# Products of probabilities and values issued for two key tiles together, in an attention and feed-forward block on one core

## The reference, cut to what matters

```python
x = x + attention(layernorm(x))          # x is 1 x 4096 x 256, float32
x = x + ffn_fp8(layernorm(x))            # 256 x 256 weight, rounded to fp8 values

def attention(x):                        # 16 heads of 16 columns, causal over 4096 rows
    q, k, v = split(x @ Wqkv_w + Wqkv_b)
    attn = softmax(q @ k.T * 0.25 + causal_mask)
    y_softmax = attn @ v
    # recurrence over the rows: state = retention*state + Gamma * outer(v_t, k_t)
    y_stp = scan(state, (q, k, v))       # y_t = (W_static + state) @ q_t
    alpha = sigmoid(gelu(x @ gate_w1 + gate_b1) @ gate_w2 + gate_b2)
    return (alpha * y_softmax + (1 - alpha) * y_stp) @ out_w + out_b
```

## Time and profile before

| | |
|---|---|
| median of three runs | 2258.62 us (2258.2 to 2261.62) |
| the profiled execution, span from first to last instruction | 2262.8 us |
| TensorE busy, share of the span | 2012.1 us, 89% |
| VectorE busy | 1911.7 us, 84% |
| ScalarE busy | 1258.6 us, 56% |
| GpSimd busy | 838.2 us, 37% |
| mean granted TensorE clock | 0.940 of full speed |

### The profile page before, as it was taken

How to read it: one execution, slowest core, us unless ns; L and a number is a source line. 1 busy time by engine, 2 the same in 40 slices (tenths; PEclk the granted TensorE clock), 3 DMA queues, 4 the chain that set the end, 5 groups by cost and what they waited for, 6 DMA issues and landing times. The chain is left out here.

```text
span 2262.8 us, 42161 instructions
## 1 busy us (share of the span) xinstructions
PE 2012.1 (89%) x11840; PEld 696.9 (31%) x11840; DVE 1911.7 (84%) x3051; ACT 1258.6 (56%) x2518; POOL 838.2 (37%) x843
## 2 busy tenths in 40 slices
PE   6876999999989999999898999989999999998543
PEld 3441233323323332333223333232332322222432
DVE  5656999998997999989987999898979898863677
ACT  3532166665655666666556666665656666766221
POOL 1320042433443433425342424253514242754435
PEclk9985599999999999999999999999999999999775
DMA  5987152251132622512235314221452111211702
GB/s 142 266 188 168 23 95 49 66 88 57 44 82 56 103 64 57 90 49 62 59 71 101 73 50 67 68 62 53 88 79 75 47 45 38 68 44 35 198 28 74
DMA packets 153963, 179.50 MB, mean 79 GB/s; under 512 B 62352, under 2 KB 100240, under 8 KB 153744
## 3 DMA queue, kind: packets, MB, share of 16 engines
q1 hardware_dynamic: 151360, 175.06, 33.2%
q10 hardware_dynamic: 2384, 1.77, 0.3%
HBM read 134.32 MB, written 42.21 MB: 78 GB/s over the span
## 5 line engine op out<-in xcount | busy, mean ns | idle before, releaser
L1004 DVE TENSOR_REDUCE pmax<-PS 128x1 f32<-128x512 f32 (+3 forms) x2304 | 1335.1, 635 | 181.9 <-PE PS L860 123.2
L971 ACT ACTIVATE probs<-PS 128x512 f32<-128x512 f32 (+3 forms) x2304 | 1118.0, 567 | 615.3 <-PE PS L878 481.6
L860 PE MATMUL PS<-K_st,Q_st 96*128 96x512 bf16 (+3 forms) x1408 | 502.3, 362 | 32.9 <-DVE pmax L1004 28.9
L878 PE MATMUL PS<-Q_st,K_st 98*128 98x512 bf16 (+3 forms) x1408 | 443.2, 361 | 16.5 <-ACT probs L971 11.3
L824 POOL COPY carry<-state 128x1 f32<-128x1 f32 x256 | 47.1, 184 | 1061.9 <-DVE state L1040 1061.9
L860 PE MATMUL PS<-K_first,Q_st 96*128 96x512 bf16 (+3 forms) x896 | 354.2, 411 | 64.9 <-DVE pmax L1004 34.0
L835 POOL TENSOR_TENSOR v_exp<-v_exp,k_rows 128x512 f32<-128x512 f32 x256 | 348.2, 1361 | 108.4 <-DMA v_exp<-qkv_t 108.2
L1040 DVE TENSOR_TENSOR_SCAN state<-retention,carry,v_exp 128x512 f32<-128x512 f32 x256 | 357.1, 1395 | 1.8 <-POOL v_exp L835 1.6
L899 PE MATMUL PS<-probs,V_g 128*17 128x512 f32 (+3 forms) x2816 | 343.5, 561 | 0.0
L826 POOL TENSOR_TENSOR state<-state,q_rows 128x512 f32<-128x512 f32 x256 | 330.5, 1291 | 20.6 <-POOL carry L824 0.2
L878 PE MATMUL PS<-Q_st,K_first 98*128 98x512 bf16 (+3 forms) x896 | 298.7, 373 | 7.2 <-issue 6.2
(11 more groups left out here) (124 smaller groups left out, 999.0 us busy)
## 6 DMA issues: line engine op xcount, KB each, us to landing
v_exp<-qkv_t SPq DMA_DIRECT2D x256, 256.0 KB
qkv_t<-proj SPq DMA_DIRECT2D x24, 512.0 KB, 3.5
qk_parts<-parts SPq DMA_DIRECT2D x24, 512.0 KB, 4.7
Q_st<-qk_parts SPq DMA_DIRECT2D x192, 64.0 KB, 3.9
K_first<-qk_parts SPq DMA_DIRECT2D x24, 320.0 KB, 12.6
K_st<-qk_parts SPq DMA_DIRECT2D x24, 320.0 KB, 13.6
K_st<-qk_parts SPq DMA_DIRECT2D x24, 192.0 KB, 6.8
v_rows<-vaug SPq DMA_DIRECT2D x32, 136.0 KB, 5.9
```

What stands on the lines that cost most here:

```text
L860: mm = pe.matmul(PS[:, bank, 0:width], Q_st[0:KS, c, h, j * P:(j + 1) * P], keys[0:KS, h, blk * CH:blk * CH + width], start=True, stop=(bl ...
L878: mm = pe.matmul(PS[:, bank, 0:CH - r * P], keys[:, h, kt * P:(kt + 1) * P], Q_st[:, c, h, r * P:CH], start=True, stop=(kt < TPC * c))
L971: act.activation(probs[:, tile % P_SLOTS, h, 0:CH - r * P], PS[:, item % S_BANKS, 0:CH - r * P], ACT.Exp, scale=SCALE).then_inc(exp_done, 1)
L1004: dve.tensor_reduce(pmax[:, s % 2, hj, blk:blk + 1], PS[:, S_BANKS + item % M_BANKS, 0:width], AX.X, ALU.max).then_inc(max_done, 1)
```

## The change

The planner keeps the tiles whose V is due in a list, and issues V for two tiles together. With tiles counted from 0, V of tiles t-2 and t-1 now stand after the fourth S of tile t for every even t from 2 on, and odd tiles have no V. `probs` gets a fourth buffer (8 KB more of each partition). The evacuation of a finished chunk (`out_evac`) and its turn stay behind the last V of the chunk; since all chunks have an even number of tiles, that V is issued in the same tile as before. At the end of a group the last two V are issued together, as before. V itself, its waits, and every other step are unchanged.

```diff
-P_SLOTS = 3
+P_SLOTS = 4
+TOGETHER = 2
...
-    pending = None
+    pending = []
+
+    def values_of(tiles):
+        for tile in tiles:
+            emit(("values", 0) + tile)
+            if tile[1] == KEY_TILES[tile[0]] - 1:
+                emit(("out_evac", 0, tile[0]), event=False)
+                if tile[0] < NCH - 1:
+                    turns.append([6, ("out_turn", 0, tile[0]), 5, ("out_norm", 0, tile[0])])
+
...
-            if pending:
-                emit(("values", 0) + pending)
-                if pending[1] == KEY_TILES[pending[0]] - 1:
-                    emit(("out_evac", 0, pending[0]), event=False)
-                    turns.append([6, ("out_turn", 0, pending[0]), 5, ("out_norm", 0, pending[0])])
-            pending = (s, kt)
+            if len(pending) == TOGETHER:
+                values_of(pending)
+                pending.clear()
+            pending.append((s, kt))
             max_items(share[GH])
     assert not slots and not todo
-    emit(("values", 0) + pending)
-    emit(("out_evac", 0, NCH - 1), event=False)
+    values_of(pending)
```

## The result

| | before | changed |
|---|---|---|
| median of the runs | 2260.12 us (four runs, 2258.2 to 2264.89) | 2401.09 us (four runs, 2392.57 to 2414.42) |
| ratio, 95% interval | | 1.062 (1.057 to 1.066) |
| span of the profiled execution | 2262.8 us | 2406.8 us (2408.49 us as a run) |

The change makes the kernel 6.2% slower. The forecast was 2368 us, range 2300 to 2408; the median lies in the range, near its upper end, and two of the four runs (2408.49 and 2414.42) lie above it.

The account below looks back on a forecast made before the run. TensorE was taken to bound pairs without units, VectorE the commoner pairs with them. Three full groups at +28 (+84) and the fourth at +25 gave +109 on the 2262.8 us span; the median forecast was 2368 us, range 2300 to 2408.

Parts of the forecast that it names:

- The loop: From the M behind one pair of V to the next, through VectorE and three banks: 6.95 us, 6.80 with narrow blocks.
- 32 pairs, unit on the odd tile, up to tile 72: Pairs in each group where VectorE runs dry across both V: +0.80 us each, less diagonal savings, +23 us.
- nine more beyond tile 80: Pairs in groups 1 to 3 with four M a tile and a unit on the odd tile alone: 0.7 each, +6 us.
- the fourth group: Last group: +22 up to tile 80 with bursts' saving, then ScalarE's loop adds +4; in all +25 us.
- pairs without a unit: 0: Pairs of tiles with no unit: TensorE's saving is used up by the loop, bounds -0.2 and +0.1 us.
- the -1 for the tiles behind the bursts: Tiles behind each burst, with four S and V and no M, keep the saved switch: 4 x 0.23, -1 us.
- these M are too few to bind the banks: Fourth group beyond tile 80: M mostly too few for the banks to bind, so ScalarE's loop does; +4 us on 28 pairs.
- more is late: Rival: late evacuations (28 us) or a lower clock from TensorE's longer waits, 2410 to 2440 us; chance 0.09.
- the rival that the pair is not cheaper: Rival: the second V has its own drain of 0.21 us, loop 7.01, 33 us more, 2401 us; chance 0.05.
- ScalarE's loop in the fourth group: Beyond tile 80, exponentials, S and both V form a loop of 5.42 us a pair, +0.12 to +0.15 on 28 pairs.
- Smaller loss: Rival: present stalls at narrow blocks, folds and turns are absorbed by VectorE's new idle time, 2300 to 2325 us; chance 0.17.
- TensorE's saving is the gain: Rival: VectorE never runs dry, so up to 61 us of saved switches come back, some 2198 or 2230 us; chance 0.07.

Follow-up runs that it names:

- pairs_at_units: Changed kernel with V paired only where a unit stands ahead of a tile with four M, elsewhere single: 2245.03 us, 0.992 of the kernel before.

## Why the prediction was right, and where it was off

The direction, the mechanism and its price per pair were right. The loop was forecast at 6.95 us for whole blocks and 6.80 on average; it is 6.90 in the rows above, and over the 32 pairs with a unit up to tile 72 the mean length is 6.75. (This and the sums below are from the starts of the first S of each tile; for each pair the shortest of its three occurrences in the full groups, which leaves most of the disturbances below aside.)

| a full group | forecast | measured |
|---|---|---|
| 32 pairs, unit on the odd tile, up to tile 72 | +23 | +24.9 |
| nine more beyond tile 80 | +6 | +6.4 |
| all other pairs | -1 | +2.4 |
| sum | +28 | +33.7 |
| the fourth group | +25 | +27.2 |

Three groups and the fourth make +128, against the +109 forecast. The step that was mis-sized most is "pairs without a unit: 0" with its companion, the -1 for the tiles behind the bursts. A pair without a unit went up by 0.07 to 0.13 (tiles 73 to 76), about the upper bound given for it, and those at a chunk's end or behind a burst by 0.35 to 0.42 (5.23 to 5.58 us at tiles 33 and 34, 5.21 to 5.63 at 39 and 40). After the change these take 5.58 to 5.79 us, about what the loop without a scan was walked at, 5.61 to 5.76; what the prediction had wrong is that all of them took 5.69 before. Only two of four bursts kept the saved 0.23.

The prediction and the text ahead of it say that the fourth group has three M a tile beyond tile 80 and then two. By the list it has two from tile 80, one from 117 and none from 136. The step that hangs on it, that these M are too few to bind the banks, holds all the more.

The remaining 16 us of the span's +144 have no place in the sum. About 9 of them are pairs that were longer than their like. One is seen here, tiles 25 and 26 of the second group, a window and the M and V in it:

```profile
861.20:869.53 8.33, 6.70 (x33) 1.82 (x31) 5.87 (x11) 4.10 (x8) 2.67 (x3) 0.80 0.22 58
```

```profile
863.98 0.39 PE L867 MATMUL PS<-K_st,Q_st 96*128 96x512 bf16 x1 [1.64 <-DVE pmax L1011]
...
865.98 3.39 PE L906 MATMUL PS<-probs,V_first 128*17 128x512 f32 x16
```

The granted clock of this window is 0.80, part of it at 1.2 instead of 2.4 GHz, and V lasts 3.39 us instead of 1.91. The pairs of the three full groups exceed the shortest of their kind by 17.0 us in all, by 7.6 before, and the granted clock over the span is 0.933 after 0.940. In the clock record of the traces, attention has 17 falls to the lower level after the change, 75 us in all, and 8 before, 27 us. Of the 17.0 us, 15.4 are in pairs that ran partly at the lower level; of the 7.6, 3.5. Some pairs ran partly at it in all three groups, so that its cost is in the table too. Tiles 125 and 126 went from 6.59 to 8.80 us (10.34 in the first group), tiles 119 and 120 from 6.64 to 8.25, while 133 and 134, which had run partly at it in all three groups before, fell from 9.11 to 6.84. Tiles 125 and 126 of the third group, before and after:

```profile
1601.40:1608.22 6.82, 5.84 (x33) 1.59 (x32) 6.40 (x10) 4.13 (x8) 4.74 (x5) 1.00 0.80 153
```

```profile
1714.46:1723.27 8.81, 7.01 (x34) 1.94 (x33) 6.01 (x9) 4.13 (x8) 4.34 (x5) 0.81 0.82 123
```

So the rival "more is late" had a part in it: ahead of the fall in the tiles 25 and 26 TensorE had waited 1.64 us for VectorE's bank, and its clock fell more often. That the waits are what lowers it was not tested by itself. Its other form, late evacuations, doesn't show: no pair at a chunk's end or behind it (looked at up to tile 90: tiles 15 to 18, 35 to 38, 59 to 62, 87 to 90) grew beyond the 6.91 of the loop, but for two that were longer before and grew shorter. Another 4 us of the 16 lie behind attention, whose work is the same, and some 2 ahead of it and between the groups.

The other steps: the second V costs 0.87 and the switch comes once, as read from narrow tiles: both V take 1013.71 to 1015.55, 1.84 us, which is 0.87 + 0.99 less 0.02; the rival that the pair is not cheaper fell. ScalarE's loop in the fourth group came out at 5.48 us a pair, 5.42 to 5.45 forecast. The fourth buffer cost nothing, as said. "Smaller loss" was partly true: the pairs that had stalls at a fold or a turn (6.46 and 6.27 us at tiles 17 and 19) rose by 0.44 and 0.33 only, but there are too few.

The rival "TensorE's saving is the gain" asked for a backlog of VectorE, which was not there in the changed kernel. `pairs_at_units` joins V only where a scan lies among VectorE's last pieces of work: 152 pairs of the 288, 32 us of TensorE's time at 0.21 each, and the kernel gains 17.

## What to carry to other kernels

Two engines that hand buffers to each other in a ring can be bound by a loop, and not by either's busy time: from the first product behind a long foreign job, through the consumer, back to the last one ahead of it. Before merging foreign jobs to save a switch, add up that loop, with every piece of the consumer's other work that stands in it, and compare it with the busier engine's own time; a job of the consumer's that stands inside the gap fills time in which it would be idle, and the same job elsewhere in the loop lengthens the loop by all of it (here a scan of 1.19 us: pairs of 6.91 with it in the loop, 5.79 without a unit, 5.94 with the unit moved). Walk the loop for the list as a whole: two gaps with one hand-over between them are nearly one gap.

## What the runs showed of the hardware

The V of four heads run side by side, each in its strip of the array: in the pair at 1006.80 the four first matmuls start within 0.02 us, and the second four 0.43 us later. A first V behind an M, with the way back to M, costs 1.08 us, one behind another V 0.87. The 0.21 between them is what going from the full array to strips and back costs here; M and V also differ in type (bf16 and float32), and no run separates the two.

Of the 71 pairs of tiles that lie within a group, 63 before the change and 62 after it take the same time within 0.02 us in all three full groups (6.91 in each). In seven of the nine exceptions after the change the granted clock falls, which takes 0.7 to 2.5 us at once. Others, such as tiles 71 and 72 before the change (7.14 us once, 6.05 otherwise), stand out at a clock of 1.00, and their cause was not looked for. In the rows above, a reader started 0.42 us after the start of a 512-column matmul, VectorE and ScalarE alike. A bank that was freed was written 0.05 to 0.06 us later.
